# Cross keys stored once and copied on the way back in, and a shorter list of waits before the first transposes

## What is computed

```python
x = x + self_attention(_layernorm(x), Wqvk, Wo)          # 16 heads of 8, causal
x = x + cross_attention(_layernorm(x), ctx_768, Wq, bq, Wk, bk, Wv, bv, Wo, bo)
x = x + mixture_of_experts(_layernorm(x), ...)           # 8 experts of 512, the top 2 of a row

# in cross_attention
k = (key_value @ Wk + bk).reshape(B, Nkv, H, D).transpose(0, 2, 1, 3)
v = (key_value @ Wv + bv).reshape(B, Nkv, H, D).transpose(0, 2, 1, 3)
attn = jnp.einsum('bhqd,bhkd->bhqk', q, k) * scale        # then clip, softmax over 6404 keys, @ v, @ Wo + bo
```

## Time and profile before

| | us |
|---|---|
| median of 3 runs | 1050.58 |
| lowest and highest | 1050.01, 1050.95 |
| the profiled execution | 1049.28 |
| its span, first to last instruction | 1047.5 |
| TensorE busy | 889.7 (85%) |
| ScalarE busy | 878.2 (84%) |
| VectorE busy | 173.3 (17%) |
| moved by DMA | 48.64 MB, 46 GB/s on average |

### The profile page before, as it was taken

One profiled execution on the slowest core, in us unless ns is written; L12 is line 12 of the kernel. 1 busy time (PEld: TensorE's weight loads), 2 busy tenths in 40 slices (PEclk: granted clock), 3 DMA queues, 4 the chain that ended last, 5 costly groups with the idle time before them and its releaser, 6 DMA issues.

```text
span 1047.5 us, 14492 instructions
## 1 busy us (share of the span) xinstructions
PE 889.7 (85%) x6144; PEld 260.0 (25%) x6144; DVE 173.3 (17%) x520; ACT 878.2 (84%) x682; POOL 12.8 (1%) x37
## 2 busy tenths in 40 slices
PE   5976888999888888888888888888888888399998
PEld 3552222222111111111111111111111111144443
DVE  5744663431000000000000000000000000421112
ACT  3645897999999999999999999999999999144443
POOL 3000000100000000000000000000000000000000
PEclk9985899999999999999999999999999999799999
DMA  4393007100111110011001011001110000000000
GB/s 137 125 335 109 1 1 244 44 31 31 34 36 58 34 33 31 31 40 57 31 33 34 31 64 33 31 31 33 34 61 1 1 1 1 2 1 0 1 0 21
DMA packets 19364, 48.64 MB, mean 46 GB/s; under 512 B 3058, under 2 KB 6492, under 8 KB 19292
## 3 DMA queue, kind: packets, MB, share of 16 engines
q1 hardware_dynamic: 19292, 47.63, 13.8%
HBM read 33.99 MB, written 13.64 MB: 45 GB/s over the span
## 4 chain that ended last, share of the span: by engine, by line
issue 31%; PE 31%; ACT 30%; DVE 3%; SPq 3%; DMA 1%; ACTq 0%; DVEq 0%
ACT probs L656 30%; PE psum L1266 9%; PE psum L1500 6%; PE psum L1489 5%; PE psum L1238 5%; SPq L430 3%; PE psum L1138 1%; PE psum L1382 1%; DVE turned L886 1%; PE psum L1262 1%; DMA ctail<-in_ctx 1%; PE psum L1482 1%; PE psum L1171 0%; PE psum L1175 0%; PE psum L1159 0%
## 5 line engine op out<-in xcount | busy, mean ns | idle before, releaser
L656 ACT ACTIVATE probs<-psum 128x1536 f32<-128x1536 f32 (+1 forms) x515 | 782.9, 1827 | 34.2 <-PE psum L1238 14.3
L1266 PE MATMUL psum<-probs,v_ctx 128*9 128x512 f32 x3200 | 422.5, 601 | 2.8 <-DVE turned L886 2.8
L1238 PE MATMUL psum<-q_all,k_ring 32*128 32x512 f32 (+1 forms) x1792 | 263.6, 495 | 110.0 <-ACT probs L656 104.5
L1238 PEld LDWEIGHTS psum<-q_all,k_ring 32*128 32x128 f32 x1792 | 102.4, 186 | 508.6 <-ACT probs L656 460.6
L886 DVE STREAM_TRANSPOSE turned<-psum 128x512 f32<-128x512 f32 x16 | 11.5, 717 | 660.7 <-PE psum L1262 644.5
L710 ACT ACTIVATE probs<-psum,b_sb 128x512 f32<-128x512 f32 x64 | 44.0, 687 | 64.4 <-PE psum L1489 64.3
L1266 PEld LDWEIGHTS psum<-probs,v_ctx 128*9 128x9 f32 x3200 | 47.9, 88 | 105.1 <-issue 99.7
L1500 PE MATMUL psum<-probs,ctx_region 128*128 128x512 f32 x128 | 66.5, 604 | 0.0
L1489 PE MATMUL psum<-xnT,w_region 128*128 128x512 f32 x128 | 65.5, 595 | 0.0
L1266 PE MATMUL psum<-probs,v_self 128*9 128x512 f32 (+3 forms) x384 | 43.0, 550 | 3.1 <-DVE turned L886 2.0
L1489 PEld LDWEIGHTS psum<-xnT,w_region 128*128 128x128 f32 x128 | 24.0, 190 | 30.3 <-issue 26.9
(11 more groups left out here) (151 smaller groups left out, 288.2 us busy)
## 6 DMA issues: line engine op xcount, KB each, us to landing
k_ring<-kc_parts SPq DMA_DIRECT2D x16, 832.0 KB, 4.4
k_ring<-kc_parts SPq DMA_DIRECT2D x16, 768.0 KB, 4.2
kc_parts<-kparts_bc SPq DMA_DIRECT2D x32, 256.0 KB, 3.8
kc_parts<-probs SPq DMA_DIRECT2D x16, 256.0 KB, 3.6
w_region<-in_L_ffn_W SPq DMA_DIRECT2D x1, 2048.0 KB, 13.3
ctx_region<-in_ctx SPq DMA_DIRECT2D x1, 768.0 KB, 9.1
ctx_region<-in_ctx SPq DMA_DIRECT2D x1, 672.0 KB, 7.7
ctx_region<-in_ctx SPq DMA_DIRECT2D x1, 576.0 KB, 6.5
```

What stands on the lines that cost most here:

```text
L656: act.activation(probs[:, slot:slot + w, :], psum[:, at:at + w, :], ACT.Exp, scale=SC[ph]).then_inc(L[ph]["exp_done"], 1)
L1238: mm = pe.matmul(into[:, col:col + n_q], keys, q_all[rows, g, hf * HALF + q0:hf * HALF + q0 + n_q], start=True, stop=True)
L1266: mm = pe.matmul(into[:, q0:q0 + w], v_all[:, h, t, :], probs[:, place(ph, at)[1], col:col + w], start=first, stop=last)
```

## The change

`kc_parts` gets the form (PARTS, D, KV): both parts of all 128 features, each once. A chunk is stored in one transfer of both parts, 128 partitions x 2 x 512 columns. The copies are made by the loads: a piece is loaded in 16 transfers, one for each of 4 heads and 4 copies, into 8 partitions each. ktail is loaded the same way in 16 transfers, and now behind pieces 0 and 1 instead of ahead of them. Waits on these semaphores count 16 x 16 a piece, and 16 instead of 64 a stored chunk. ctail gets a semaphore of its own, for which TensorE waits at the last chunk only. The wait for the four small loads of wk, bk, wv, bv moves behind the transposes of chunks 0 and 1. The general path's load of a head's keys becomes four transfers.

```diff
-        kc_dram = nc.dram_tensor("kc_parts", (H * ROWS, KV), F32).ap()
+        kc_dram = nc.dram_tensor("kc_parts", (PARTS, D, KV), F32).ap()
...
-            sp.dma_start(ctail[:, :], ctx[0, KT * P:KV, :]).then_inc(s["wctx_loaded"], 16)
+            sp.dma_start(ctail[:, :], ctx[0, KT * P:KV, :]).then_inc(s["ctail_loaded"], 16)
...
-                for part in range(PARTS):
-                    for copy in range(2):
-                        at = (2 * part + copy) * HD
-                        sp.dma_start(kc_rows[:, at:at + HD, c * CHUNK * P:c * CHUNK * P + w], kparts[c % KRING][:, part, 0:w])\
-                            .then_inc(s[f"kctx_stored{c % KRING}"], 16)
+                sp.dma_start(kc_dram.rearrange("i p c -> p i c")[:, :, c * CHUNK * P:c * CHUNK * P + w],
+                             kparts[c % KRING][:, :, 0:w]).then_inc(s[f"kctx_stored{c % KRING}"], 16)
...
-                sp.dma_start(k_ring[:, slot * PIECE:slot * PIECE + (b - a) * P].bitcast(F32),
-                             kc_dram[g * P:(g + 1) * P, a * P:b * P]).then_inc(s[f"k_loaded{slot}"], 16)
-
-            sp.dma_start(ktail[:, :, :], kc_dram.rearrange("(g p) c -> p g c", p=P)[:, :, KT * P:KV])\
-                .then_inc(s["ktail_loaded"], 16)
+                for r in range(LANES):
+                    h = LANES * g + r
+                    for j in range(COPIES):
+                        row = ROWS * r + HD * j
+                        sp.dma_start(k_ring[row:row + HD, slot * PIECE:slot * PIECE + (b - a) * P].bitcast(F32),
+                                     kc_dram[j // 2, h * HD:(h + 1) * HD, a * P:b * P]).then_inc(s[f"k_loaded{slot}"], 16)
+
             for load in range(K_SELF_PIECE):
                 load_piece(load)
+            for r in range(LANES):
+                for j in range(COPIES):
+                    row = ROWS * r + HD * j
+                    sp.dma_start(ktail[row:row + HD, :, :],
+                                 kc_dram[j // 2].rearrange("(g r d) c -> r d g c", g=QUADS, r=LANES)[r, :, :, KT * P:KV])\
+                        .then_inc(s["ktail_loaded"], 16)
...
                 if c == NCHUNK - 1:
+                    pe.wait_ge(s["ctail_loaded"], 16)
...
             pe.wait_ge(s["ident_made"], 1)
-            pe.wait_ge(s["wctx_loaded"], 16 * 5)
             for c in range(2):
                 transpose_ctx(c)
+            pe.wait_ge(s["wctx_loaded"], 16 * 4)
             pe.wait_ge(s["ones_made"], 2)
             project_ctx(0)
```

More of the change, by code:

```diff
@@ L350, in decoder_layer @@
         for name in (
-            "x_loaded0 x_loaded1 wself_loaded ctx_loaded0 ctx_loaded1 ctx_loaded2 ctx_loaded3 wctx_loaded wlate_loaded wffn_loaded "
+            "x_loaded0 x_loaded1 wself_loaded ctx_loaded0 ctx_loaded1 ctx_loaded2 ctx_loaded3 wctx_loaded ctail_loaded wlate_loaded wffn_loaded "
             "ident_made rows_made consts_made outs_cleared ones_made low_made bq_made dve_step wself_quads wcross_quads "
@@ L421, in _ @@
                         .then_inc(s["wlate_loaded"], 16)
-            kc_rows = kc_dram.rearrange("(h x) c -> h x c", x=ROWS)
             for c in range(NCHUNK):
@@ L426, in _ @@
                 sp.wait_ge(s["kctx_split"], c + 1)
-                for part in range(PARTS):
-                    for copy in range(2):
-                        at = (2 * part + copy) * HD
-                        sp.dma_start(kc_rows[:, at:at + HD, c * CHUNK * P:c * CHUNK * P + w], kparts[c % KRING][:, part, 0:w])\
-                            .then_inc(s[f"kctx_stored{c % KRING}"], 16)
+                sp.dma_start(kc_dram.rearrange("i p c -> p i c")[:, :, c * CHUNK * P:c * CHUNK * P + w],
+                             kparts[c % KRING][:, :, 0:w]).then_inc(s[f"kctx_stored{c % KRING}"], 16)
             for n in range(KRING):
-                sp.wait_ge(s[f"kctx_stored{n}"], 64 * len(range(n, NCHUNK, KRING)))
+                sp.wait_ge(s[f"kctx_stored{n}"], 16 * len(range(n, NCHUNK, KRING)))
             def load_piece(load):
@@ L454, in general_head_loop @@
                     sp.wait_ge(G[ph]["round"], h * NBLK + 1)
-                    sp.dma_start(k_gen[ph].bitcast(F32), k_dram[bass.ds(h * ROWS, ROWS), :]).then_inc(G[ph]["kq"], 16)
+                    if ph == 0:
+                        sp.dma_start(k_gen[0].bitcast(F32), k_dram[bass.ds(h * ROWS, ROWS), :]).then_inc(G[0]["kq"], 16)
+                    else:
+                        for j in range(COPIES):
+                            sp.dma_start(k_gen[1][HD * j:HD * j + HD, :].bitcast(F32),
+                                         k_dram[j // 2, bass.ds(h * HD, HD), :]).then_inc(G[1]["kq"], 16)
                     with sp.Fori(0, NBLK) as b:
@@ L617, in ctx_keys @@
                 if c >= KRING:
-                    act.wait_ge(s[f"kctx_stored{c % KRING}"], 64 * (c // KRING))
+                    act.wait_ge(s[f"kctx_stored{c % KRING}"], 16 * (c // KRING))
                 evac(kparts[c % KRING][:, 0, 0:w].bitcast(F32R), bank(2 + c % 2)[:, 0:w], s["kctx_first"])
@@ L688, in _ @@
             for n in range(KRING):
-                act.wait_ge(s[f"kctx_stored{n}"], 64 * len(range(n, NCHUNK, KRING)))
+                act.wait_ge(s[f"kctx_stored{n}"], 16 * len(range(n, NCHUNK, KRING)))
             choose(act, 0, lambda: exponentials(0), lambda: general_exponentials(0))
@@ L1041, in _ @@
             heads_turned(1)
-            dve.wait_ge(s["ktail_loaded"], 16)
+            dve.wait_ge(s["ktail_loaded"], 16 * LANES * COPIES)
             dve.tensor_tensor(ktail_quads[:, :].rearrange("p (g x) -> p g x", g=QUADS)[:, :, 0:LANES * TAIL]
@@ L1235, in score_group @@
                             if r == 0 and t == t0:
-                                pe.wait_ge(s[f"k_loaded{slot}"], 16 * (load // PIECE_RING + 1))
+                                pe.wait_ge(s[f"k_loaded{slot}"], 16 * LANES * COPIES * (load // PIECE_RING + 1))
                             keys = k_ring[rows, slot * PIECE + (t - t0) * P:slot * PIECE + (t - t0 + 1) * P]
@@ L1301, in general @@
                         n = h * NBLK + b
-                        pe.wait_ge(G[ph]["kq"], (h + 1) * 16)
+                        pe.wait_ge(G[ph]["kq"], (h + 1) * (16, 16 * COPIES)[ph])
                         pe.wait_ge(G[ph]["q"], (n + 1) * 16)
```

## The result

| | before | after |
|---|---|---|
| median (lowest to highest), us | 1050.3 (1047.57 to 1050.95), 4 runs | 1035.61 (1035.17 to 1038.11), 4 runs |
| profiled execution, us | 1049.28 | 1035.95 |
| span, us | 1047.5 | 1034.2 |
| ratio after to before | | 0.9885, 95% interval 0.9865 to 0.9905 |
| HBM written, MB | 13.64 | 7.08 |

The changed kernel is faster by 1.15%, 12.1 us by the ratio (10.0 to 14.2), 13.3 by the two profiled executions and 14.7 by the medians. The forecast was 10.9 us, 1039.7, with a range from 1035.3 to 1045. Measured again later (e11), the same kernel came to 0.9909 of before, 9.5 us less (6.9 to 12.1).

What follows compares the result with a forecast made beforehand. The prediction took the stores to bound the stage before the attention and the exponentials the cross attention. Gains of 3.4 + 5.1 + 2.4 = 10.9 us, with narrow loads costing nothing, gave 1050.58 - 10.9 = 1039.7 us, range 1035.3 to 1045.

Steps and rivals of the forecast that it cites:

- The bound: Before the attention begins the stage is bound by the stores; the change can give time only in the first 84 us.
- Part 1: Start: TensorE's first transposes wait only for the context's first part, until VectorE's normalised rows end next; gain 3.4 us.
- the 0.9 us that were to cost nothing: Start: the context's first part, taken to land in 3.6 us, could land 0.9 us later at no cost.
- 2.8 if the clock were still low: Start: lower value of the first wait's 3.4 us gain, should TensorE's clock still be low; upper end 4.7.
- Part 2: Context chunks 6 to 12: one store a chunk instead of four, 2.19 us a step, 13.14 instead of 18.27; gain 5.1 us.
- its slack in the ring: Chunk ring: a store may take 5.2 us from issue to landing before its slot is needed; 4 was taken.
- the DMA engines were the full resource, not only SyncE: Chunk stage: argument for the rival that stores still pace the ring, 1046.0 us, chance 0.15 (stores pace or part of it).
- Part 3: Last chunk to first exponential: TensorE's chain is next instead of the last store, 9.1 instead of 11.56 us; gain 2.4 us.
- the step 76.99 to 81.28: Before the first exponential: from VectorE's norm columns to the first scores, 4.29 us, expected to stay.
- Part 4: Piece loads: 16 transfers of 8 rows, 10 us of issue against 22.6 us a reload, hidden; cost nothing until 1.41 us each.
- The sum: Whole kernel: 3.4 + 5.1 + 2.4 = 10.9 us gained, from 1050.58 to 1039.7 us.
- a clock that stays up in the first self scores: First 25 us of self attention: rival with TensorE held at 2.4 GHz, 5.4 us more, 1034.3 us; chance 0.13.

Runs made afterwards that it cites:

- e11: The changed kernel measured again, unchanged, in the later job: 0.9909 of before (0.9884 to 0.9934), median 1036.93 us.
- e6: Changed kernel with each narrow load cut into 6 by columns, 96 transfers a piece instead of 16, same bytes: 1343.8 us, run once.
- e1: Kernel before with only the waits moved (ctail's own semaphore, small loads' wait behind the first transposes): 0.9986 of before, 1045.38 us.
- e3: Changed kernel with every chunk stored a second time to an unread DRAM tensor, two 512 KB transfers a chunk: 0.9948 of before.
- e4: Changed kernel with each chunk's store cut into four transfers of 128 KB, same bytes: 0.9941 of before.
- e7: Changed kernel with 28 unused matmuls of 128 columns on TensorE ahead of the context's first transposes: 0.9894 of before.
- e8: Changed kernel with 4 unused matmuls of 512 columns on TensorE ahead of the first scores: 0.9916 of before.
- e9: Changed kernel with TensorE's wait for the cleared output bank moved behind the first two score groups: 1030.98 us, 0.9865 of before.
- e12: e9 plus unused matmuls: 22 ahead of the context's first transposes, 5 between the halves of the normalised rows: 0.9860 of before.
- e10: Changed kernel with unused matmuls before the first transposes, between the normalised rows' halves and behind the first eight self score groups: 0.9927 of before.

## Why the prediction was right, and where it was not

- **The bound.** Right: the stores bound the chunks' stage, and most of the gain lies there. From c1 to the first exponential 8.1 us went.
- **Part 1, the waits: 3.4 forecast, 1.4 measured in the first profile, 2.0 to 2.2 against before in most others, 3.7 in one.** The chain was right: TensorE at 8.60 (the context's first part took 4.5 us to land, not 3.6, within the 0.9 us that were to cost nothing), VectorE's rows at 15.53 as the next limit. The mis-sized term is the lower bound, "2.8 if the clock were still low". I had charged the low clock to four transposes only. The four projections behind them also ran at 1.2 GHz, 3.62 us instead of 1.88. In the first profile, and in e6 (3.49 us), they fall into the time before the clock has risen; before, they came after it. In seven others with the early start (e1, e3, e4, e7, e8, e9, e12) the clock had risen already, as the first four transposes took 0.60 us. Then TensorE idled 1.8 to 2.4 us for VectorE's second half, and the four projections took 2.9 to 3.3 us. Where the idle stretch was 1.2 us (e11) or filled (e10) they took 1.88. So either way the low clock took back 1.2 to 2 us of what the wait gave, in all but e10 and e11, and the forecast's 3.4 or a little more comes through without it (3.7 in e11).
- **Part 2, the stores: 5.1 forecast, 5.4 measured** (31.10 to 25.66). The steps took 2.19 us. The store landed in 2.8 us where I took 4, so its slack in the ring was 2.4 us and not 1.2. The 0.3 more came at the last step, 1.86 us, as the last chunk is a short one (260 columns). Which of bytes and issues bounded I had left open ("the DMA engines were the full resource, not only SyncE"); e3 and e4 show that both did.
- **Part 3, to the first exponential: 2.4 forecast, 2.6 measured**, 8.94 us where I had 9.1. The next limit was the one named, TensorE behind VectorE's columns, and the step 76.99 to 81.28 came back as 68.97 to 73.24. What held TensorE in it was the clearing of the output bank, as e9 showed.
- **Part 4, the narrow loads: nothing forecast, nothing measured.** A narrow load took 0.35 us of SyncE's time, not 0.62, so a piece took 5.5 us, not 10. At half of the 306 GB/s the bytes of a piece were to take 5.6 us; they moved at 100 GB/s, so about 8.5 us, an estimate, is nearer, and it is the longer of the two. Both are hidden in 22.6 us, so the error cost nothing. The Trainium skill, page "DMA: Bandwidth & Descriptors", section "Why a DMA increments its semaphore by 16 and not by 1", gives 8 engines for 8 rows; the trace agrees, with a DMA share of 0.51. The rule of the Trainium skill (the same page, section "Rules for kernel authors") against transfers under 64 KB did not decide the time here, as the loads are hidden; what they cost is seen in the rate.
- **The sum.** 10.9 us forecast to the first exponential, 9.5 in the profile. The further 3.8 us that took the profile to 13.3 lie behind the first exponential, in a stretch that scatters from 955.4 to 960.9 us over 13 profiles, both ends with the new stores. I had put this into the range from one cause only, a clock that stays up in the first self scores. It did not; the 1.5 us at the start of the cross attention and most of another 1.5 at its end came from the clock in other places. So the profiled 13.3 us are no larger effect of the change. By the ratio, 12.1 us (10.0 to 14.2), the forecast is inside the interval, and by e11's, 9.5 us (6.9 to 12.1), too. That the median of 1035.61 fell inside the range, 0.3 us above its lower end, is partly luck: two of its four runs were below 1035.3, and the median of before, 1050.3 here, was 1046.0 to 1048.8 in the later measurements.

## What to carry to other kernels

When a stage is bound by its stores, count both prices of a chunk, the bytes at the full rate and the issues on the queue: here they lay within a microsecond, and halving the issues alone gave 2.7 us (e3) and halving the bytes alone 4.0 (e4), of the 8.1 that both gave. Copies that a reader can make cheaply need not be stored. On the reading side hold two prices against the length of a step, the number of issues (0.35 us each) and the bytes at the rate of narrow transfers (100 GB/s here, against 423 for wide ones). Before a first wait is shortened, ask which state TensorE's clock is in when the work starts earlier, and compare profiles by stretches, since a single pair can differ by 4 us in places that the change doesn't touch.

## What I had not expected of the hardware

- The granted clock can read 1.00 in the first 20 us although the work shows 1.2 GHz. In the profile after, four matmuls of 512 columns took 3.62 us from 16.49 on in a stretch with the clock at 1.00, and 1.88 us at 20.95. In e7, where the clock had risen and fallen before, the same stretch reads 0.63. The durations are to be believed there.
- A store of 512 KB from 128 partitions landed in 2.8 us, while 256 KB took 3.8 in the full queue before and 512 KB took 5.8 in the median behind another in e3. A landing time is a property of the queue as much as of the size.
- The issue of one transfer on SyncE: 0.37 us for a store of both parts in one, 0.60 for a quarter of it by 64 partitions in e4, 0.30 for an 8-row load, with 0.35 from one such load to the next.
- Loads of 8 rows moved at some 100 GB/s with a DMA share of 0.51, loads of 128 rows at 423 GB/s with 1.01: half of the engines, and a quarter of the rate.
